# A gated delta rule on one core: one block inverse for the four token tiles of a call in place of two

## What is computed

```python
q = _l2norm(_causal_dw_conv_silu(x @ Wq, conv_q))   # k the same; v without the norm
beta = sigmoid(x @ Wb) * 2; alpha = exp(-exp(A_log) * softplus(x @ Wa + dt_bias))
def step(state, inp):
    q_t, k_t, v_t, a_t, b_t = inp
    retained = einsum('bhvk,bhk->bhv', state, k_t)
    state = a4 * (state - b4 * retained[..., None] * k_t[:, :, None, :]) + b4 * v_t[..., None] * k_t[:, :, None, :]
    o_t = einsum('bhvk,bhk->bhv', state, q_t)
    return state, o_t
out = out * rsqrt(mean(out * out) + 1e-5) * o_norm_w * silu(x @ Wg)
```

## Time and profile before

| | |
|---|---|
| runs | 3619.95 us median (3609.34 to 3629.92) |
| profiled execution, span | 3635.6 us |
| PE busy | 3157.9 us (87%) |
| DVE busy | 2261.0 us (62%) |
| ACT busy | 1429.1 us (39%) |
| POOL busy | 932.4 us (26%) |
| costliest group | L570, 345.3 us of PE |
| costliest DVE group | L663, 286.0 us |
| chain that ended last | PE 66%, DVE 18%, ACT 5%, issue 4%, DMA 3% |

### The profile page before, as it was taken

How to read it: one execution, slowest core, us unless ns; L and a number is a source line. 1 busy time by engine, 2 the same in 40 slices (tenths; PEclk the granted TensorE clock), 3 DMA queues, 4 the chain that set the end, 5 groups by cost and what they waited for, 6 DMA issues and landing times.

```text
span 3635.6 us, 86922 instructions
## 1 busy us (share of the span) xinstructions
PE 3157.9 (87%) x35006; PEld 2198.3 (60%) x35006; DVE 2261.0 (62%) x5812; ACT 1429.1 (39%) x3328; POOL 932.4 (26%) x851
## 2 busy tenths in 40 slices
PE   5689988888898888898868989876889999999989
PEld 5367666666676666766657867665445545544544
DVE  6566778666778666678446645635546556556555
ACT  1544444444444444344136622124333433433331
POOL 0112231412222412222405526432212212221110
PEclk7898988899998899899679989988879999999999
DMA  6111211302111301211347754285111111111000
GB/s 239 41 37 45 66 47 30 130 28 63 57 49 48 118 26 49 60 49 38 101 152 187 195 164 137 93 257 178 40 41 42 35 42 47 36 41 43 5 18 18
DMA packets 224091, 280.89 MB, mean 77 GB/s; under 512 B 35072, under 2 KB 172464, under 8 KB 223312
## 3 DMA queue, kind: packets, MB, share of 16 engines
q1 hardware_dynamic: 184448, 216.93, 18.4%
q0 software_dynamic: 34896, 54.20, 6.7%
q10 hardware_dynamic: 4352, 4.20, 0.3%
HBM read 184.64 MB, written 90.62 MB: 76 GB/s over the span
## 4 chain that ended last, share of the span: by engine, by line
PE 66%; DVE 18%; ACT 5%; issue 4%; DMA 3%; POOL 1%; DVEq 0%; ACTq 0%; SPq 0%; POOLq 0%
PE banks L3054 6%; PE banks L570 5%; DVE s_d_kq L663 3%; PE banks L1940 3%; PE banks L2589 3%; PE banks L809 2%; PE banks L1282 2%; PE banks L2575 2%; PE banks L1949 2%; PE banks L2601 2%; PE banks L796 2%; PE banks L970 2%; PE banks L968 2%; PE banks L2845 2%; PE banks L2755 2%
## 5 line engine op out<-in xcount | busy, mean ns | idle before, releaser
L570 PE MATMUL banks<-s_d_xT,s_w_qkvg 128*128 128x512 f32 x640 | 345.3, 667 | 14.8 <-DVE s_d_kq L663 9.6
L663 DVE SCALAR_TENSOR_TENSOR s_d_kq<-banks,s_conv_w,s_d_kq 128x511 f32<-128x511 f32 (+2 forms) x384 | 286.0, 745 | 53.2 <-ACT s_d_kq L615 43.4
L2717 ACT ACTIVATE s_g_pT<-banks 128x1536 f32<-128x1536 f32 (+1 forms) x96 | 152.8, 1592 | 365.7 <-PE banks L2591 365.7
L3054 PE MATMUL banks<-s_m_we,s_m_tT 128*128 128x512 f32 x512 | 234.5, 603 | 6.0 <-DVE s_m_x L3117 6.0
L615 ACT ACTIVATE s_d_kq<-banks,s_conv_w 128x512 f32<-128x512 f32 x128 | 87.9, 687 | 282.1 <-PE banks L570 281.5
L641 ACT ACTIVATE s_d_square<-banks 128x128 bf16<-128x128 f32 x512 | 134.6, 278 | 158.6 <-PE banks L599 158.4
L570 PEld LDWEIGHTS banks<-s_d_xT,s_w_qkvg 128*128 128x128 f32 x640 | 125.6, 210 | 117.5 <-issue 90.0
L1940 PE MATMUL banks<-s_q_xsT,s_q_w 128*128 x1008 | 162.1, 285 | 37.0 <-issue 27.9
L2674 DVE TENSOR_REDUCE s_g_off<-banks 128x4 f32<-128x512 f32 (+2 forms) x96 | 117.2, 1220 | 123.0 <-PE banks L2575 120.9
L1940 PEld LDWEIGHTS banks<-s_q_xsT,s_q_w 128*128 128x128 f32 x1008 | 156.2, 199 | 60.2 <-issue 47.3
L796 PEld LDWEIGHTS banks<-s_d_Xc,s_d_Mc 32*32 32x32 f32 x8192 | 92.2, 115 | 129.5 <-DVE s_d_Xc L909 54.8
(11 more groups left out here) (415 smaller groups left out, 7714.7 us busy)
## 6 DMA issues: line engine op xcount, KB each, us to landing
s_q_w<-w12p SPq DMA_DIRECT2D x128, 257.0 KB, 6.3
s_q_xs<-xs SPq DMA_DIRECT2D x32, 516.0 KB, 5.6
s_d_E<-sums SPq DMA_DIRECT2D x64, 256.0 KB, 3.4
s_r_xT<-xfT SPq DMA_DIRECT2D x12, 1024.0 KB, 7.0
tree<-s_r_bias SPq DMA_DIRECT2D x96, 128.0 KB
s_r_work<-xf SPq DMA_DIRECT2D x24, 512.0 KB, 4.5
og<-s_d_o SPq DMA_DIRECT2D x16, 512.0 KB, 3.0
sorted<-s_q_acc SPq DMA_DIRECT2D x32, 256.0 KB, 2.1
```

Source lines behind the costliest of these rows:

```text
L570: ins = e.matmul(bk[6 + j % 2][:], w[:, par, c, self.COL[what] + h * P:self.COL[what] + (h + 1) * P], xT[:, c, :], start=(c == 0), stop=(c ...
L663: e.scalar_tensor_tensor(d[:, a:], bk[6 + j % 2][:, 0:SEQ - a], cw[:, par, k0 + 3 - a:k0 + 4 - a], d[:, a:], ALU.mult, ALU.add).then_inc(s ...
L2717: e.activation(self.pT[c][:], psum[:, 0:4, 0:self.COLUMNS[c]], ACT.Exp).then_inc(self.exped, 1)
L3054: ins = e.matmul(self.product_bank(b, k, q)[:], self.tT[:, c, t * P:(t + 1) * P], self.we[:, c, (2 * half + q) * 512:(2 * half + q + 1) * ...
```

## The change

One inverse is computed for the four tiles of a call, with operations 512 wide in place of 256, and ten setup steps (`SETUP = 10`), then six levels of four steps. Level 5 is done in turned form: besides X's lower block, Z^T is made directly by products with the operands changed (L801 to L803 of the kernel after), so that the transposes by TensorE fall away; ScalarE copies the pieces into Pf. M's diagonal blocks are read in place by the level products; D is made in the tile of the decays, which is now doubled for whole calls, loaded by SP at step 19 and made by GpSimd at step 23. `UNREAD` is zero throughout, and the product after level 6's first is gone. The whole walk of call n-1, four tiles and the norm, stands beside the first 18 steps of the inverse of call n; of the last call all four tiles are walked with nothing beside them. S, R, U and T1 are parts of one tile, `walked`, which the output's squares overwrite, so that the clear of S (L1046) waits for the norm of the call before. The squares of k and q share one tile.

```diff
-        self.E = two("E", [P, H, P])
-        self.Dm = [sb(f"d_DD{j}", [P, H, P]) for j in range(4)]
-        self.Pf = two("Pf", [P, 2, H, P])
-        self.S, self.R, self.U, self.T1 = (sb(n, [P, H, 64]) for n in ("d_S", "d_R", "d_U", "d_T1"))
+        self.XT6 = sb("d_XT6", [P, TPB * H, 64])
+        self.X6, self.T6 = self.XT6[0:64], self.XT6[64:P]
+        self.Dm = two("DE", [P, TPB, H, P])
+        self.walked = sb("d_walked", [P, 4, H, 64])
+        self.S, self.R, self.U, self.T1 = (self.walked[:, j] for j in range(4))
...
-    UNREAD = (0, 0, 0, 1, 2, 2)
+    UNREAD = (0, 0, 0, 0, 0, 0)
+    SETUP, LEVEL = 10, 4
...
+        for h in (2 * half, 2 * half + 1):
+            c0 = (h % 2) * 256
+            ins = e.scalar_tensor_tensor(self.M[:, H * t + h, :], bank[:, c0:c0 + P], kd[:, 2, t, h:h + 1], E[:, h, :], ALU.mult, ALU.mult)
+        ins.then_inc(self.M_made, 1)
+        e.wait_ge(self.M_made, 8 * n + 2 * t + half + 1)
+        e.tensor_tensor(E[:, 2 * half:2 * half + 2, :], bank[:].rearrange("p (h a n) -> p h a n", h=2, a=2)[:, :, 1, :], E[:, 2 * half:2 * half + 2, :], ALU.mult).then_inc(self.D_made, 1)
...
-                    ins = e.matmul(bk[2][r, 32 * a:32 * a + 32], XT[r, a, :], TB[r, a, :], start=True, stop=True)
+                else:
+                    e.matmul(bk[2][0:32, c], TB[32:64, a, :], XT[32:64, a, :], start=True, stop=True)
+                    e.matmul(bk[2][64:96, c], TB[96:P, a, :], XT[96:P, a, :], start=True, stop=True)
+                    ins = e.matmul(bk[2][32:64, c], XT[32:64, a, :], TB[32:64, a, :], start=True, stop=True)
...
-        for c in range(2):
-            for h in range(H):
-                ins = e.transpose(bk[1 + c][:, h * P:(h + 1) * P], X[:, c, h, :], g.ident[:])
-            ins.then_inc(self.X_turned, 1)
-        yield
-        self.idle_tensor(e)
...
             if l == 5:
-                self.split_scalar(e, m)
+                e.wait_ge(self.Xc_made, 6 * n + 6)
+                e.wait_ge(self.zeroed, 2)
+                for b in range(2):
+                    ins = e.activation(self.block(X6, b, b), self.Xc[32 * b:32 * b + 32], ACT.Copy)
+                ins.then_inc(self.X6_diagonal, 1)
+                e.wait_ge(self.XT_made, 5 * n + 5)
+                e.wait_ge(self.Uh, 4 * n)
+                self.diagonal_scalar(e, 1)
...
+        for half in range(2):
+            e.wait_ge(self.T_made, 7 * n + 6 + half)
+            e.activation(self.T6[:, 8 * half:8 * half + 8], bk[half][64:P].rearrange("p (a n) -> p a n", n=64), ACT.Copy).then_inc(self.B_made, 1)
+        self.diagonal_scalar(e, 0)
+        yield
+        if n + 1 < self.CALLS:
+            self.decays_scalar(e, n + 1)
...
-            if n:
-                e.wait_ge(self.stepped, 28 * n)
-            e.memset(self.S[:], 0.0).then_inc(self.S_zero, 1)
+        if n:
+            e.wait_ge(self.o_normed, 4 * n - 3)
+        e.memset(self.S, 0.0).then_inc(self.S_zero, 1)
...
-            ahead = project(e, n + 1) if n + 1 < self.CALLS else iter(())
-            main, here = invert(e, n, 0), state(e, n, 0)
-            side_by_side((next(main) for _ in range(6)), (last, 0.5), (ahead, 0.67))
-            side_by_side(main, (last, 0.64), (ahead, 0.8), (beside, 0.62))
+            ahead, main = project(e, n + 1) if n + 1 < self.CALLS else iter(()), invert(e, n)
+            side_by_side((next(main) for _ in range(self.SETUP)), (last, 1.2), (ahead, 0.9), (beside, 0.5))
+            side_by_side((next(main) for _ in range(2 * self.LEVEL)), (last, 2.3), (ahead, 1.6), (beside, 1.0))
             finish(last)
-            main = invert(e, n, 1)
-            side_by_side((next(main) for _ in range(6)), (ahead, 1.34))
-            side_by_side(main, (here, 0.5), (ahead, 0.8), (beside, 0.62))
-            finish(here, ahead)
-            last = state(e, n, 1)
+            side_by_side(main, (ahead, 1.8), (beside, 1.0))
+            finish(ahead)
+            last = state(e, n)
```

More of the change, by code:

```diff
@@ L105, in __init__ @@
         self.g, keep = g, g.keep
-        g.ident, g.upper, g.ones = (keep(n, [P, P]) for n in ("ident", "upper", "ones"))
+        g.ident = keep("ident", [P, P])
         g.mask, g.eye = keep("mask", [P, 5, 32], U32), keep("eye", [P, 32])
@@ L900, in invert_vector @@
+    def invert_vector(self, e, n):
+        g, bk, Xc, XT = self.g, self.g.bank, self.Xc, self.XT
+        mask = lambda l: g.mask[:, l, None, :].broadcast_to((P, TPB * H, 32))
+        yield
+        for t in range(TPB):
+            for half in range(2):
+                self.setup_vector(e, n, t, half)
+                if (t, half) != (3, 1):
+                    yield
+        e.wait_ge(self.M_made, 8 * n + 8)
         for b in (0, 1):
@@ L957, in state_tensor, with invert_gpsimd @@
-    def state_tensor(self, e, n, pair):
+    def invert_gpsimd(self, e, n):
+        if n == 0:
+            e.memset(self.X6, 0.0).then_inc(self.zeroed, 1)
+            e.memset(self.Pf[:], 0.0).then_inc(self.zeroed, 1)
+            e.wait_ge(self.zeroed, 2)
+        else:
+            e.wait_ge(self.X6_low, n)
+            e.wait_ge(self.X6_diagonal, n)
+        e.tensor_copy(self.Xc[:], self.g.eye[:, None, :].broadcast_to((P, TPB * H, 32))).then_inc(self.eye_set, 1)
+        for step in range(self.SETUP + 6 * self.LEVEL):
+            if step == 23 and n + 1 < self.CALLS:
+                self.decays_gpsimd(e, n + 1)
+            yield
@@ L998, in state_vector @@
         flat = lambda t: t[:].rearrange("p t h v -> p (t h) v")
-        for t in (2 * pair, 2 * pair + 1):
+        for t in range(TPB):
             s = 4 * n + t
```

437 lines of the change are left out of this document (187 added, 250 removed).

## The result

The changed kernel takes 3829.99 us (median of 4, 3826.99 to 3840.76), the kernel before 3614.72 us beside it: a ratio of 1.0575, 95% interval [1.0532, 1.0618]. It is slower by 215 us, where 3591 was forecast; the time lies outside the range and on the other side. The profiled execution has a span of 3826.1 us.

What follows compares the result with a forecast made beforehand. TensorE was taken to bound the delta stage at 105.8 us a call; stretches 55.7 + 19.2 + 21.7, routing 1.5 + 1.5 and clock 4.4 gave 104.0, −25 us over 14 calls, ends −4: 3591 us, range 3500 to 3695.

Steps and rivals of the forecast that it cites:

- routing, both terms: Routing's remaining products and steps inside the second and third stretches: 1.5 us a call on TensorE and 1.5 on VectorE.
- clock: TensorE after 12.6 empty us: products at half clock at the start of setup and walk, 4.4 us more a call.
- price of leaving out the unread products: Levels 3 to 6: 22 unread products a call, .21 us each, go, counted as −4.7 us a call.
- rival B: Delta stage slower: clock stays at half through setup, walk and levels; 111 us a call, 3689 us; chance .25.
- point of decision: Delta stage: the kernel gets slower once the loss by the clock passes 6.5 us a call.
- Stretch 1: First walk product to T of level 3: VectorE ends last by little, 55.7 us a call.
- Stretch 2: T of level 3 to TB of level 5: TensorE bounds, 14.4 us of products and 4.8 of waits, 19.2.
- Stretch 3: TB of level 5 to the next walk product: ScalarE's chain 18.3 us, then GpSimd's 3.4, 21.7 in all.
- The bound of 25: Upper end for TB of level 5 to the next walk, if routing's gathers on GpSimd hold it up: 25 us.
- Products: TensorE's products in the delta stage fall by 5.7 us a call, from 84 to 78.
- Ends: Start of call 0 +3 us; last call −31 for its levels and +24 for two uncovered tiles; together −4.

Runs made afterwards that it cites:

- e1: The kernel before with its 22 unread products a call left out and nothing else changed: ratio 1.015 [1.007, 1.023] to the kernel before.
- e2: The changed kernel with 21 unread products a call put back in levels 3 to 6: 1.0406 to the kernel before, against 1.0427 for the changed kernel.
- e13: The changed kernel with S cleared by VectorE in the norm before and the routing moved out of the last stretch: 1.0330 to the kernel before.
- e14: The changed kernel with S cleared by VectorE, the routing moved and the 21 unread products a call put back: 1.0217 to the kernel before.
- e16: The changed kernel with VectorE's clear, the routing moved and the projection's rates at 1.2 in levels 1 and 2 and 2.1 after: 1.0211 to the kernel before.
- three edits of the boundary: The changed kernel with S cleared by VectorE, projection rate 2.3 in the last 16 steps and the exps behind the root: 1.0235 to the kernel before.
- one of them: The changed kernel with only the clear of S moved to VectorE, inside the output norm of the call before: 1.0121 to the kernel before.
- e12: The kernel before with twice as many unread products in levels 3 to 5, 20 more a call: 1.0043, +16 us.

## Why the prediction was wrong

Mean of calls 1 to 14 in the changed kernel, in us, beside the forecast's stretches:

| stretch | forecast | measured | TensorE waits | at full | at half |
|---|---|---|---|---|---|
| 1, walk to T3 | 55.7 | 67.8 | 9.5 | 38.4 | 19.9 |
| 2, T3 to TB5 | 19.2 | 26.4 | 7.0 | 11.3 | 8.6 |
| 3, TB5 to the walk | 21.7 | 25.8 | 9.5 | 4.4 | 11.4 |
| routing, both terms | 3.0 | in the above | | | |
| clock | 4.4 | in the above, 19.9 | | | |

**The step that failed is the clock.** It was put at 4.4 us a call, 5 less than before, with the words that the clock "will be low for the start of the setup and the walk, and rise once the wide projections follow". By the same count that gives 9.9 before, it is 19.9 (18.0 with each shape at its own price): 14 to 15 us a call beyond the forecast, which missed the repeat by 15 (104.0 and 119.2). That the two agree is in part luck. TensorE's waits came out 4.5 us above what the forecast's own sums leave for them (104.0 − 78.3 − 4.4 = 21.3), and the work 4.9 below its 78.3, and these two cancel. The clock is low in all three stretches, at .79 on the mean.

Two first stretches of the changed kernel show what it does. Calls 2 and 7 have the same products but for four of the routing (1.7 us at full clock), the same busy time of VectorE (42.9 and 43.2 us) and the same waits of TensorE (7.0 and 6.9): call 2 takes 54.8 us with 3.4 us of products at half, call 7 64.1 with 20.5. Call 10 above (68.7 us, 28.5 at half) has twelve products of the routing more than call 2, some 5 us of the difference. Calls 4, 9 and 14 are another case, with the products of call 2 but 58 us of VectorE's work: they take 70 to 77 us, with 14 to 17 of waits.

Within the step, the term with the wrong sign was the price of leaving out the unread products. It was counted as −4.7 us a call; it is +4 in the kernel before (e1's repeat and ratio), about nothing in the changed one (e2), and +2.3 once the boundary is cleared (e13 and e14). That is 5 to 9 of the 15 us by experiment. The rest of the clock's cost is read from the records, and no run here brought it back as a whole. The forecast's only thought of this price stood in rival B.

Rival B had the side and the mechanism, with 111 us a call and 3689 us; it was still 141 us short, since it left the waits as forecast and the clock's cost at 11.4. Its point of decision (6.5 us a call) was passed threefold, and its signs (a clock under .85 with a repeat over 107) both came. The boundary with its gaps runs at .50 to .61, and with the levels ahead of it filled at 1.00. The Trainium skill's rule ("TensorE: Matmul & The Clock Gate", "HAM oscillation — how this bites in real kernels") that idle gaps between products bring half clock agrees with that. Gaps alone don't tell the whole here: the first stretch of call 10 stands at .79 with TensorE busy 94% of it, and call 2's at .95 with 87%.

**Stretch 1:** the length without the clock came out near (9.5 + 38.4 + 19.9 / 2 = 57.9 for 55.7), and that is luck, for the reason was wrong. VectorE does not end last in it: it is busy 43 to 58 us of 55 to 77, 48.5 on the mean where 54.6 were summed. TensorE's work is 48.4 where some 52 were taken, and its waits add 9.5. So TensorE's products and the chain between the two set the stretch; e16 shows that VectorE's queue has a share, 3.6 us of waits with the rates changed. The copies and transposes of 512 columns took .70 to .73 us where .78 was taken.

**Stretch 2:** waits 7.0 for 4.8, and 8.6 us at half clock, for which the forecast had nothing here.

**Stretch 3:** right in its parts, 21.8 us in four of 14 calls and 21.2 to 25.2 in six more. What it lacked are the calls in which a wait for the routing's scatter stands in VectorE's queue (4, 9 and 14, 30 to 38 us; call 1 has 29 us by the routing's products), 4 us a call on the mean. The bound of 25 had put such a delay on GpSimd's queue alone. It was both: VectorE behind a DMA holds up the root, and in calls 4 and 14 GpSimd's scatters hold up the clear by 6.7 us after it.

**Products:** the work fell by 10.1 us a call by that count (9.4 with each shape at its own price), 5.7 were forecast. What the rest is, no run here shows.

**Ends:** +14.2 at the start for +3, and −10.7 for −7 at the end: the two further tiles cost 12.06 us each, as in the earlier trace rows. At the start 8.4 of the 14.2 lie in call 0's inverse, in which TensorE waits 19.7 us for 9.7 before and is at half clock for 44 us for 17. The table load is followed by the first exp without a drain here too (819.45 + 1.28 is 820.73, the exp starts at 820.74), so the rule of the Trainium skill ("ScalarE: Activation LUTs") was rightly given nothing.

Left open: what keeps the clock low in a first stretch that TensorE fills to 94%, why three edits of the boundary stand at 1.0235 in their median and one of them at 1.0121 while their profiled executions agree, and what in the chips makes the kernel before 3% slower on two of them. Spreading the walk over more levels was not tried.

## What to carry to other kernels

Price a product that nobody reads by the clock with and without it, not by its own time: in the kernel before, 4.7 us of them a call saved about 9 (e1). How much they save hangs on the order around them: about their own time in the changed kernel (e2), and a second set bought no clock at all (e12). Merging two half-wide frames into one wide frame saves few products and leaves one boundary a call at which every engine's leftover work stands in a row with nothing beside it; put what the next frame's first product needs (a clear, a norm) on an engine whose queue is empty there. And step through the queue of each engine at a boundary for work of another stage that waits for a DMA: three calls in fourteen paid 8 to 16 us, behind a copy of four columns on VectorE and a row of scatters on GpSimd.

## What the hardware showed that was not expected

The granted clock of one and the same program differs from chip to chip: over the whole kernel before it was .915 on the mean, with 3610 and 3621 us, on two of them, and .90, with 3714 to 3717 us, on two others. The delta stage's time at half clock was 20.3 us a call on the first and 25.2 on a slower one, while VectorE's operations kept their durations (745 ns for L663 on both). The clock is not all of it: half of the 4.4 us a call between them is waits of TensorE. A comparison across chips by time would have been off by 100 us, about half of the effect studied.
